# Attention block on one core: who issues the DMAs of the head, tables loaded once, and a tail in four batches

## The reference

```python
x = hidden_states                      # 1 x 1024 x 512, float32
q = (x @ w_q)                          # 32 heads of 128
k, v = x @ w_k, x @ w_v                # 8 heads of 128, each shared by 4 query heads
lq = x @ w_lq                          # 128 wide
lk, lv = lq @ w_lk, x @ w_lv           # 32 heads of 128
q, k, lk = rope(q), rope(k), rope(lk)
out = causal_attn(q, k, v) @ w_o + causal_attn(q, lk, lv) @ w_lo
x = layernorm(x + out)
logits = x @ route_w.T                 # 8 experts; the best one is taken, weighted by its logit
h = x @ A[e].T                         # 8 experts of rank 16
y = (one_hot(argmax) * max * h) @ Bw
x = layernorm(x + y)
```

## Time and profile before

| | us |
|---|---|
| median of 3 runs | 1983.04 (1981.39 to 1983.26) |
| the profiled execution | 1982.13 |
| its span, first to last instruction | 1979.6 |
| PE busy in the span | 1949.8 (98%) |
| DVE / ACT / POOL busy | 1348.5 / 1032.7 / 1128.6 |

### The profile page before, as it was taken

The page is one execution under the profiler, slowest core; times in us unless marked ns, Lnnn a source line. Parts: engine busy times, 40 slices in busy tenths (PEclk is TensorE's granted clock), DMA queues, the critical chain, the costliest instruction groups (busy, mean ns, idle before and its releaser), DMA issues.

```text
span 1979.6 us, 30315 instructions
## 1 busy us (share of the span) xinstructions
PE 1949.8 (98%) x11104; PEld 1727.1 (87%) x11104; DVE 1348.5 (68%) x3242; ACT 1032.7 (52%) x2335; POOL 1128.6 (57%) x904
## 2 busy tenths in 40 slices
PE   7999999999999999999999999999999999999997
PEld 5989889898898988989898898988989888898985
DVE  5757757576675857757487584766757577575766
ACT  3654627456273653727447273563726547274564
POOL 4647566474754756556475564756546565564750
PEclk8999999999999999999999999999999999999999
DMA  7030120302103030030400203021040300303001
GB/s 265 1 129 3 40 102 12 120 1 101 41 12 120 1 126 16 12 120 1 142 0 27 105 1 141 1 89 43 1 141 1 118 14 18 125 2 116 1 12 43
DMA packets 53074, 117.03 MB, mean 59 GB/s; under 512 B 6848, under 2 KB 8896, under 8 KB 52800
## 3 DMA queue, kind: packets, MB, share of 16 engines
q10 hardware_dynamic: 33936, 69.21, 9.6%
q1 hardware_dynamic: 18992, 45.90, 7.0%
HBM read 108.81 MB, written 6.29 MB: 58 GB/s over the span
## 4 chain that ended last, share of the span: by engine, by line
PE 96%; ACT 2%; DVE 1%; ACTq 1%; POOL 0%; issue 0%; DMA 0%; SPq 0%
PE ps L438 28%; PE ps L440 27%; PE ps L439 27%; PE ps L526 13%; ACT probs L719 1%; ACTq L749 0%; DVE probs L974 0%; ACT acc L794 0%; PE ps L641 0%; PE ps L626 0%; POOL pt_lo L875 0%; ACT k_hi L685 0%; ACT val_hi L685 0%; DMA acc<-xT 0%; DVE stats L1042 0%
## 5 line engine op out<-in xcount | busy, mean ns | idle before, releaser
L903 POOL TENSOR_TENSOR probs<-probs,inv_sum 128x640 f32<-128x640 f32 (+7 forms) x512 | 584.4, 1147 | 383.8 <-DVE inv_sum L981 383.7
L974 DVE CUSTOM_DVE_ANT_0 probs<-ps,mask 128x640 f32<-128x640 f32 (+7 forms) x512 | 383.5, 751 | 68.8 <-PE ps L440 63.4
L719 ACT ACTIVATE probs<-probs,neg_max 128x640 f32<-128x640 f32 (+7 forms) x512 | 398.0, 778 | 52.6 <-DVE neg_max L974 47.5
L915 DVE TENSOR_TENSOR pt_lo<-ps,pt_hi 128x512 fp32r<-128x512 f32 (+3 forms) x512 | 269.2, 549 | 156.5 <-ACT pt_hi L685 156.5
L526 PE MATMUL ps<-ident,probs 128*128 128x128 f32 x2304 | 335.7, 273 | 0.0
L685 ACT ACTIVATE pt_hi<-ps 128x512 fp32r<-128x512 f32 (+3 forms) x512 | 234.3, 489 | 184.2 <-PE ps L526 184.2
L685 ACT ACTIVATE ql_hi<-probs 128x512 fp32r<-128x512 f32 x128 | 81.0, 633 | 439.1 <-POOL probs L894 439.1
L526 PEld LDWEIGHTS ps<-ident,probs 128*128 128x128 f32 x2304 | 274.5, 140 | 27.4
L894 POOL TENSOR_TENSOR probs<-probs 128x512 f32<-128x512 f32 x144 | 186.4, 1295 | 167.6 <-DVE probs L951 167.5
L438 PE MATMUL ps<-val_hi,ql_hi 128*128 128x512 f32 x512 | 205.6, 401 | 0.0
L875 POOL TENSOR_TENSOR pt_lo<-raw,pt_hi 128x1024 fp32r<-128x1024 f32 (+1 forms) x47 | 94.3, 2021 | 191.3 <-ACT pt_hi L685 191.3
(11 more groups left out here) (109 smaller groups left out, 4435.7 us busy)
## 6 DMA issues: line engine op xcount, KB each, us to landing
x_hi<-x_kept ACTq DMA_DIRECT2D x30, 1024.0 KB, 8.8
x_lo<-x_kept ACTq DMA_DIRECT2D x30, 1024.0 KB, 12.2
raw<-wo SPq DMA_DIRECT2D x32, 512.0 KB, 3.6
raw<-wq SPq DMA_DIRECT2D x16, 512.0 KB, 3.9
raw<-wlv SPq DMA_DIRECT2D x16, 512.0 KB, 4.5
raw<-wkv SPq DMA_DIRECT2D x8, 512.0 KB, 7.5
acc<-xT SPq DMA_DIRECT2D x4, 512.0 KB, 6.0
wlk_raw<-wlk SPq DMA_DIRECT2D x16, 128.0 KB, 3.4
```

The lines of the kernel that those rows point to most:

```text
L719: nc.scalar.activation(dst, dst, ACT.Exp, bias=neg_max[:, n % 8:n % 8 + 1], scale=-1.0, accum_out=row_sum[:, n % 8:n % 8 + 1]).then_inc(q[ ...
L903: nc.gpsimd.tensor_tensor(b, b, inv_sum[:, k % 8:k % 8 + 1].to_broadcast([P, b.shape[-1]]), ALU.mult).then_inc(q["normed"], 1)
L915: return nc.vector.tensor_tensor(dst, src, h, ALU.subtract)
L974: nc.vector.tensor_tensor_reduce(out=probs_of(n).rearrange("p (b n) -> p b n", b=b), in0=scores_of(n), in1=mask[:, S - w:S].rearrange("p ( ...
```

## The change

It has two parts, and a third that the short name does not mention.

- **Head.** x is loaded in six parts (`X_PARTS`), the first and the last quarter in halves. PE runs eight products of the identity with itself (`warm_up`) as soon as the identity is made. The first w_q is split in two halves, each with its own semaphore. Each table is loaded once, in the layout in which it lies in DRAM, so PE makes 8 transposes, and eight copies by ACT (cos) and eight by DVE (sin), 64 partitions by 256 columns each, spread them over cos_t and sin_t (`table_part`, `sines`). SP, not ACT, issues the copy to x_kept and the residual, behind the loads of kv and lv0. ACT and POOL split in the order v, lv, k (before: k, v, lv).
- **Fetching x again.** SP, not ACT, issues the four DMAs of each pair, ahead of the load of lv0 (first pair of a group) or of oa1 (second pair).
- **Tail.** The batches are four of two rows, all three hand-written orders are new, and the last row's last normalisation is done by DVE (`normalize_here`) instead of ACT.

```diff
+X_PARTS = ((0, 0, 512), (0, 512, 1024), (1, 0, 1024), (2, 0, 1024), (3, 0, 512), (3, 512, 1024))
+WARM = 8
+X_BEFORE = ("lv0", "oa1")
-POOL_LO = ("q0", "k", "v", "lv0", "q1", "lv1")
+POOL_LO = ("q0", "v", "lv0", "k", "q1", "lv1")
-BATCHES = ((0, 1, 2, 3), (4, 5), (6, 7))
+BATCHES = ((0, 1), (2, 3), (4, 5), (6, 7))
+ROWS_OF_VECTOR = (7,)
...
+        def table_part(table, h, odd, top):
+
+            dst = (cos_t, sin_t)[table][top:top + HALF, 512 * h:512 * h + 512].rearrange("p (x o n) -> p x o n", o=2, n=P)
+            return (ps[HALF * odd:HALF * odd + HALF, 2 * h + table, 0:2 * P].rearrange("p (x n) -> p x n", n=P), dst[:, :, odd, :])
...
             for slot, table in ((1, cos), (2, sin)):
-                twice = probs[:, slot, 0:2 * ST * HALF].rearrange("p (t f d) -> p t f d", t=ST, f=2)
-                for f in range(2):
-                    sp.dma_start(twice[:, :, f, :], table).then_inc(q["tab_in"], 16)
+                sp.dma_start(probs[:, slot, 0:ST * HALF].rearrange("p (t d) -> p t d", t=ST), table).then_inc(q["tab_in"], 16)
...
+                        if name == X_BEFORE[pair] and (g, pair) != (0, 0):
+                            sp.wait_ge(q["pv_mm"], SEED + per_pair(g, pair, CHUNKS, 0) - CHUNKS + 6)
+                            for h in range(2):
+                                for part, dst in enumerate(x_half(h)):
+                                    sp.dma_start(dst, kept[h, part].rearrange("p (c n) -> p c n", c=CT)).then_inc(x_back[h], 16)
...
+                        if (g, name) == (0, "lv0"):
+                            sp.wait_ge(q["x_lo_made"], len(X_PARTS))
+                            for h in range(2):
+                                for part, kept_from in enumerate(x_half(h)):
+                                    sp.dma_start(kept[h, part].rearrange("p (c n) -> p c n", c=CT), kept_from).then_inc(q["x_saved"], 16)
+                            sp.dma_start(acc[:], x).then_inc(q["res_in"], 16)
...
+            def warm_up():
+                pe.wait_ge(q["const_made"], 2)
+                for _ in range(WARM):
+                    pe.matmul(ps[:, 5, 0:P], ident[:], ident[:], start=True, stop=True, skip_group_check=True)
...
+            load_landed(act, 0, "q0")
+            for a in range(2):
+                hi(parts("q0")[0][:, :, HD * a:HD * a + HD], raw_part("q0")[:, :, HD * a:HD * a + HD]
+                   ).then_inc(q["w_hi" if a else "first_hi"], 1)
...
-            act.wait_ge(q["x_lo_made"], CT)
-            nc.scalar.dma_start(acc[:], x).then_inc(q["res_in"], 16)
-            for h in range(2):
-                for part, src in enumerate(x_half(h)):
-                    nc.scalar.dma_start(kept[h, part].rearrange("p (c n) -> p c n", c=CT), src).then_inc(q["x_saved"], 16)
...
                     if pair == 0:
-                        weights_hi(g, "k")
-                    if pair == 0:
                         weights_hi(g, "v")
                     weights_hi(g, f"lv{pair}")
+                    if pair == 0:
+                        weights_hi(g, "k")
+                    if (g, pair) == (0, 0):
+                        for h in range(2):
+                            act.wait_ge(q["tab_turned"], 2 * h + 1)
+                            for top in (0, HALF):
+                                for odd in range(2):
+                                    src, dst = table_part(0, h, odd, top)
+                                    nc.scalar.activation(dst, src, ACT.Copy).then_inc(q["cos_made"], 1)
...
-                            if m == 5 and (g, pair) != (GROUPS - 1, PAIRS - 1):
-                                bring_x_back()
...
+            def sines(h):
+
+                dve.wait_ge(q["tab_turned"], 2 * h + 2)
+                for top in (0, HALF):
+                    for odd in range(2):
+                        src, dst = table_part(1, h, odd, top)
+                        if top:
+                            nc.vector.tensor_scalar(dst, src, -1.0, None, ALU.mult).then_inc(q["sin_made"], 1)
+                        else:
+                            nc.vector.tensor_copy(dst, src).then_inc(q["sin_made"], 1)
+                dve.wait_ge(q["sin_made"], 4 * h + 4)
+                dve.wait_ge(q["cos_made"], 4 * h + 4)
+                dve.wait_ge(q["tab_turned"], 4)
...
+                        if (g, pair) == (0, 0) and u < 2:
+                            sines(u)
                         if UNITS[pair][u][0] != "v" and u >= units_ahead(g, pair):
                             rope(g, pair, ROPE_UNITS[pair].index(u))
...
+            def normalize_here(y):
+                dve.wait_ge(q["chain2"], 6 * (batch_of(y) + 1))
+                nc.vector.tensor_scalar(row(y), row(y), rstd[:, y:y + 1], shift[:, y:y + 1], ALU.mult, ALU.add
+                                        ).then_inc(q["finished_here"], 1)
```

More of the change, by code:

```diff
@@ L56, with x_part_with @@
 RAW_COLS = 1024
+X_PARTS = ((0, 0, 512), (0, 512, 1024), (1, 0, 1024), (2, 0, 1024), (3, 0, 512), (3, 512, 1024))
+WARM = 8
+def x_part_with(c, n):
+    return [d == c and n0 <= n < n1 for d, n0, n1 in X_PARTS].index(True)
 SEED = 1
+X_BEFORE = ("lv0", "oa1")
 LOADS = ("q0", "kv", "lv0", "oa0", "ob0", "q1", "lv1", "oa1", "ob1")
-POOL_LO = ("q0", "k", "v", "lv0", "q1", "lv1")
-SPLIT_LAST = {"q0": "q0", "kv": "v", "lv0": "lv0", "q1": "q1", "lv1": "lv1"}
+POOL_LO = ("q0", "v", "lv0", "k", "q1", "lv1")
+SPLIT_LAST = {"q0": "q0", "kv": "k", "lv0": "lv0", "q1": "q1", "lv1": "lv1"}
 OUT_PARTS = ("oa", "ob")
@@ L427, in _ @@
             for y, t in enumerate(OUT_ORDER):
-                sp.wait_ge(q["finished"], y + 1)
+                sp.wait_ge(q["finished_here" if y in ROWS_OF_VECTOR else "finished"], [x in ROWS_OF_VECTOR for x in range(y + 1)].count(y in ROWS_OF_VECTOR))
                 sp.dma_start(out[:, t, :], row(y)).then_inc(q["stored"], 16)
@@ L671, in _ @@
             turn_x1(6, "whT_made", 5)
+            ffn(4)
             turn_x1(7, "whT_made", 6)
-            ffn(4)
             mix(6)
@@ L845, in _ @@
             normalize(2, 6)
-            normalize(2, 7)
         @block.gpsimd
@@ L1163, in _ @@
             route6(0)
+            scale4(1, 2)
             weigh(0)
+            route1(1)
+            route2(1)
+            add_last(6)
+            scale5(1, 2)
+            route3(1)
+            scale6(1, 2)
+            route4(1)
             weigh(1)
+            route5(1)
+            route6(1)
             weigh(2)
             weigh(3)
-            add_last(6)
             spread(1, 6)
-            add_ffn(0)
-            add_ffn(1)
-            spread(2, 0)
-            spread(2, 1)
@@ L1188, in _ @@
+            add_ffn(1)
+            spread(2, 1)
+            scale4(1, 3)
+            route1(2)
+            route2(2)
+            route3(2)
+            scale5(1, 3)
+            route4(2)
+            route5(2)
+            scale6(1, 3)
+            route6(2)
             weigh(4)
-            scale6(1, 2)
             weigh(5)
+            moments(2, 0)
             add_ffn(2)
+            scale1(2, 0)
+            scale2(2, 0)
+            spread(2, 2)
             add_ffn(3)
-            spread(2, 2)
+            scale3(2, 0)
@@ L1210, in _ @@
+            scale1(2, 1)
+            route4(3)
+            scale2(2, 1)
+            route5(3)
+            route6(3)
+            add_ffn(5)
+            scale3(2, 1)
             weigh(6)
             weigh(7)
-            add_ffn(5)
+            scale4(2, 1)
+            spread(2, 4)
+            scale5(2, 1)
             spread(2, 5)
-            moments(2, 1)
+            scale6(2, 1)
+            moments(2, 2)
             add_ffn(6)
-            scale1(2, 1)
+            scale1(2, 2)
+            spread(2, 6)
```

185 lines of the change are left out of this document (85 added, 100 removed).

## The result

The changed kernel takes 1969.27 us (median of 6, 1967.48 to 1971.49) beside 1982.83 for the kernel before: a ratio of 0.9933, with a 95% interval from 0.9921 to 0.9944. That is 13.6 us of the 15.6 forecast, 2.3 above the 1967 named and inside the range of 1963.8 to 1971. It is outside the band of 1964.5 to 1968.5 that had a chance of 0.66. The profiled execution was the slowest of the six: 1971.49 us around a span of 1969.3, so the two traces differ by 10.3 us where the medians differ by 13.6. Where those 3 us went is half of what follows.

What follows compares the result with a forecast made beforehand. PE was taken to set the pace between head and tail, with time to give only at these ends. Head 12.0 plus tail 3.6 made 15.6 us off, so 1967 us was named, range 1963.8 to 1971.

Steps and rivals of the forecast that it cites:

- Step 4: Head: PE's wait before the first v unit goes as ACT splits w_lk earlier and lv0 lands at 16.1; gain 8.45 us.
- step 5: Head: the v and lk units run at 2.4 GHz instead of 1.2, 2.75 us for 5.2; gain 2.45 us.
- Steps 1 and 2: Head: lq starts near 6.0 and ends at 13.9, gain 1.75 us; identity products raise the clock near 7.2, costing lq nothing.
- its last case: Head clock: products don't count as activity and the second quarter's wait breaks the rise, near 15; lq 2.6 us later.
- the first case: Head clock: identity products count as activity, the clock rises near 7.2 us and lq loses nothing.
- clock late: Rival, head: the warm-up counts for nothing, 0.8 to 2.6 us lost, up to 1969.5 us; chance 0.09.
- Step 3: Head: 16 table transposes in 1.91 us become 8; gain 1.0 us.
- Step 6: Head, behind the slow units: PE waits 1.0 us for the second rope and 1.0 for a row maximum; net loss 1.7.
- The head's sum: Head: gains of 1.75, 1.0, 8.45 and 2.45 less 1.7 for new waits; 12.0 us.
- Fetching x again: Later groups: moving the four DMAs from ACT to SP brings no gain and no loss; lv0 lands near 257 us.
- The cover: Later groups: lv's low part ends near 263 us at worst, 11 us before PE needs it.
- Tail: End of the kernel: row 7 added earlier and last normalisations shared; gain 3.5 to 3.6 us, bounds 2.0 to 4.5.

Runs made afterwards that it cites:

- e5: Kernel before, with only the issues of the copy of x and the residual moved from ACT to SP, behind lv0's load: 1974.20 us.
- e7: Changed kernel with x loaded in four parts instead of six: 1967.86 us.
- e2: Changed kernel with ten identity products ahead instead of eight, and three more behind each of the first two groups of lq matmuls: 1968.11 us.
- e1: Changed kernel without its eight identity products: 1970.21 us.
- e3: Changed kernel with the old tail (old orders, batches and last row's handling), so the head alone: 1973.66 us.
- e6: Changed kernel with x fetched again by ACT's queue at its old place instead of by SP: 1968.14 us.
- e8: e2 with the table transposes ahead of the first unit and ACT's first four cosine copies ahead of its value weights: 1966.43 us.
- e11: Changed kernel run once more with nothing altered, to see its scatter: 1969.68 us.
- e9: Changed kernel with x in four parts, 26 identity products instead of eight, and table transposes and four cosine copies ahead: 1967.48 us.
- e10: Changed kernel with x in four parts and no identity products: 1968.69 us.
- e12: Changed kernel with x in four parts, 16 identity products instead of eight, and table transposes and four cosine copies ahead: 1965.87 us.
- e4: Kernel before with the new tail alone (new orders, batches and last row's handling): 1977.61 us.

## Why the prediction was right, and where it was not

**Step 4, the stall, and step 5, the slow units.** Forecast 8.45 + 2.45 = 10.9. e5 isolates both: 9.0 us in the trace, 7.3 by medians, of which its slower tail took 1.4. There the first v unit starts 7.84 us earlier (24.15 for 31.99), 0.6 less than forecast; the rope's wait of 0.40 and 0.5 more of waits for row maxima follow, which the prediction books under step 6. The mechanism is shown: take ACT's issues away and nothing else, and the stall is gone. In the whole change both steps come out as forecast, 8.3 and 2.4 (the head's sum, below). lv0's weights were forecast for 16.1; in e7 ACT takes them at 15.06, after a wait of 0.27. The rule weighed against it in the Trainium skill (DMA: Bandwidth & Descriptors, "Issuing engines are not separate DMA queues"), that another issuing engine saves only a small issue time, does not hold for this kernel: e5 gains 7.3 us, and an issue held for 4.23 us is not small beside the 2.7 us that its 1024 KB take at 387 GB/s.

**Steps 1 and 2, the first matmul and the clock.** These are the steps that failed. I had x's second quarter split by 9.6, the clock risen near 7.2 and lq done at 13.9. Each missed. The second quarter let PE go on at 10.84, and the clock rose at 16.5. So lq was done at 17.8 (20.51 less 12 x 0.2275): 3.9 later than forecast, 2.0 later than before. Of the 3.9, 1.2 are the second quarter's lateness. The other 2.7 are the clock's: 13 of the 18 matmuls that were left ran 0.43 us apart instead of 0.2275, and e2, with the fast level there, needed 4.2 us for the 18 where the change needed 6.9. Six more slow matmuls stood ahead of a wait for x and cost nothing. The prediction had the late clock as its last case, "broken by the wait for the second quarter, near 15, 2.6 later", which is the right price; it took the first case instead, and gave the rival "clock late" 0.09. That the time fell inside the range all the same is in part luck: the head fell short by 4.7 us, and the median came out 3 us better than the trace.

The second quarter was late in every trace with six parts: ACT took it at 8.13 to 8.85 in all seven (the change, e1, e2, e3, e6, e8, e11), where four parts gave 6.53 to 8.12 (e7, e9, e10, e12) and, in the kernels before, 7.30 and 7.42, once 8.67 (e5). SP is busy with the issues of x for 2.8 to 3.2 us in six parts, for 1.85 in four. The forecast had left these two issues more at nothing. That they are the cause is not shown: no run here varied them alone, and e5 has a late quarter without them.

Side by side, the profiled executions tell what goes with the clock. With six parts and nothing in the waits, the fast level comes to stay at 16.5 (the change), 16.3 (e1), 14.1 (e3), 15.1 (e6) and 16.5 (e11), with products ahead or without. In two of the four with products (e6, e11) it had been there at 5.9 and 6.4 and was lost again. With six parts and the waits filled it is there at 8.3 (e2) and 5.9 (e8) and stays. With four parts it is there from the first lq matmul on (e7, e9, e12) if products stand ahead, and at about 12 (e10) if not. So the products ahead can lift the clock, and short waits behind them can lose it again. How much the split of x costs in time is not shown: 0.6 us by the ratios of e7 and the change, 0.3 by the medians of e7 and e6, with intervals that overlap. What is shown in time is e2 against e1, 2.1 us for products ahead and in the waits. A rule for the single wait does not come out: e7 kept the fast level over an idle time of 2.08 us, and e11 lost it behind one of 1.94 and one of 1.21. The Trainium skill (TensorE: Matmul & The Clock Gate, Part 1) has the slow clock as the default, lifted by sustained activity at a point that varies from run to run. The traces agree: e2 and e8 give PE the same work without a pause up to their first lq matmuls, which are slow in e2 (0.63 us still at 7.23) and fast in e8 (0.47 at 5.91).

**Step 3, tables.** 1.03 us of PE for 1.91, nearly as forecast. That SP is no longer held at them was no condition for step 4, by e5.

**Step 6, new waits.** Forecast: 1.0 for the rope, 1.0 for a row maximum, less 0.3. Measured: 1.37 at 29.13 and 0.84 at 50.47, and row maxima of 1.8 us in all for 1.3. By the waits that is 1.9 for 1.7; by the starts of the matmuls, the restart behind each wait included, it is 2.3. e8 shows that the rope's is a matter of order: with the tables ahead it is gone.

**The head's sum.** Forecast 12.0, measured 7.3 up to the first transposes of probabilities (64.83 to 57.55). From the starts of PE's work in the two traces:

| step | forecast | measured |
|---|---|---|
| 1 and 2, lq done | 1.75 | -2.0 |
| 3, the transposes | 1.0 | 0.9 |
| 4, up to the first v unit | 8.45 | 8.3 |
| 5, the v and lk units | 2.45 | 2.4 |
| 6, waits behind them | -1.7 | -2.3 |

So 3.8 of the 4.7 that are lacking lie in steps 1 and 2. In the profiled execution of e7, with x in four parts and all else as in the change, the head gains 11.55 (x1 at 1928.54); it was e7's fastest of five, 1.8 us under its median, so that is what the head can give and not what it usually gives.

**Fetching x again.** Nothing, as forecast, and e6 confirms it by undoing it. lv0's weights, forecast for 257, are taken by ACT at 251.84. At the second group POOL, the last two of its low parts, then PE's first use of them:

```profile
252.97 3.65 POOL L907 TENSOR_TENSOR pt_lo<-raw,pt_hi 128x1024 fp32r<-128x1024 f32 x2 [1.10 <-ACT pt_hi L719]
...
266.81 0.33 PE L464 MATMUL ps<-pt_hi,x_hi 128*128 128x384 f32 x1
```

lv's weights do come late enough to make POOL wait 1.10 us, ten before PE needs them. The cover was worked out at 11 us; it is 10.2.

**Tail.** Forecast 3.6, bounds 2.0 to 4.5. In the traces it is 4.0 to 4.1 wherever the clock holds (e4, e6, e7, e8, e10, e12: 35.4 to 35.5 us for 39.5), 3.1 to 3.2 in the changed kernel's two and in e1, 3.4 in e9 and 3.9 in e2. By medians the tail alone gave 5.0 (e4), above the bounds, with an interval from 3.0 to 6.9. The difference between the traces lies in one row. The same last stretch of PE's work, in the changed kernel:

```profile
1953.00:1958.00 5.00, 3.68 (x25) 2.72 (x23) 4.73 (x24) 0.85 (x3) 0.00 (x0) 1.00 0.02 5
1958.00:1962.00 4.00, 3.42 (x5) 0.97 (x4) 3.29 (x12) 3.46 (x7) 0.00 (x0) 0.61 0.33 125
```

and in e12:

```profile
1948.60:1953.60 5.00, 3.68 (x25) 2.74 (x23) 4.73 (x24) 0.83 (x3) 0.00 (x0) 1.00 0.02 5
1953.60:1957.60 4.00, 2.09 (x5) 0.68 (x4) 3.96 (x14) 3.46 (x7) 0.00 (x0) 1.00 0.33 125
```

Both have the same waits of 1.3 and 0.3 us ahead of the same four matmuls; in one the granted clock falls to 0.61 and the four take 3.30 us, in the other it stays at 1.00 and they take 1.96. The four take over 3 us in four of the eleven profiled executions with the new tail (the change, e1, e9, e11), 2.65 in e2 and 1.96 in the other six. e5 lost 1.4 us in the old tail in the same way, in four earlier matmuls behind a wait of 2.1. What decides it between executions is not settled; no run here took those waits away.

**Why the medians gained 3 us more than the traces.** The profiled execution of the change had the late clock in the head and the fall in the tail, and it was the slowest of six. That the faster executions of the same kernel (1967.48) lacked one of them would fit the sizes, but they weren't profiled, and this stays open.

## What to carry to other kernels

Look for engines that idle on their own DMA issues. Here an issue took 0.4 to 0.9 us on ACT until several MB stood ahead of it, then 4.23 and 3.64, and everything behind it in that engine's order waited. Give such issues to an engine whose next work is far off. And when PE starts a kernel behind its inputs, a start that is a microsecond earlier can give nothing, if the input that everything waits for next comes later by it, or if short waits keep the clock down or lose it. Put products of no use ahead and into the waits, and read the durations of the matmuls, not their start, to see what the clock did.

## What the runs showed that I had not expected

- A half quarter of x, 256 KB, did not make what follows land earlier. ACT took x's second part at 6.06 to 7.61 in the seven traces with six parts and at 6.53 to 8.12 in the four of changed kernels with four (e7, e9, e10, e12), where that part ends twice as far into x. Between executions of equal work it scatters by more than 1 us.
- The granted clock column can read 1.00 where the durations say otherwise: in the changed kernel it is 1.00 from 6 to 17 us, while matmuls take 0.63; in e11 it shows 0.50 to 0.63 from 9 to 17, with the same durations. The durations are the better witness.
- A clock that falls for the last four of PE's 11112 matmuls costs 0.85 us of the span.
